# Recurrent stage entered with one block: weights staged in the outputs' memory and split between its first steps; attention's side work moved by a slot or two, its late stores held

## What is computed

```python
def _L0_ffn_ref(x, wf, uf, bf, wi, ui, bi, wc, uc, bc, wo, uo, bo, in_c):
    def step(c, xt):
        ft = jax.nn.sigmoid(xt @ wf.T + c @ uf.T + bf)
        it = jax.nn.sigmoid(xt @ wi.T + c @ ui.T + bi)
        gt = jnp.tanh(xt @ wc.T + c @ uc.T + bc)
        return ft * c + it * gt, None
    c_final, _ = lax.scan(step, c0, x)
    return jnp.tanh(jnp.einsum('tbi,oi->tbo', x, wo) + c_final @ uo.T + bo)

def _L1_attn_ref(x, w_qkv, w_out, head_scales, head_dirs):
    ...
    scores = jnp.einsum('bhqd,bhkd->bhqk', q, k) * SCALE
    scores = jnp.where(causal[None, None], scores, -jnp.inf)
    ...
    attn = jax.nn.softmax(scores + head_scales[None, :, None, None] * geo_bias, axis=-1)
    out = jnp.einsum('bhqk,bhkd->bhqd', attn, v)
    return out.transpose(0, 2, 1, 3).reshape(Bx, Tx, Cx) @ w_out
...
h = _layernorm(x, axis=-1) * (1 + cb) + sb
x = x + gb * _L0_ffn_ref(h, ...)
...
h = _layernorm(x, axis=-1) * (1 + ca) + sa
x = x + ga * _L1_attn_ref(h, ...)
```

## Time and profile before

| | us |
|---|---|
| median of 3 runs | 2527.28 (2520.66 to 2527.5) |
| the profiled execution | 2525.71, span 2523.9 |
| PE busy in it | 2237.5 (89%) |
| DVE / ACT / POOL busy | 1622.1 / 1315.0 / 435.3 |
| recurrent stage, first DMA to last instruction | 664.5 to about 1027 |
| attention, batch loop | 1121 to about 2000 |

### The profile page before, as it was taken

The page is one execution under the profiler, slowest core; times in us unless marked ns, Lnnn a source line. Parts: engine busy times, 40 slices in busy tenths (PEclk is TensorE's granted clock), DMA queues, the critical chain, the costliest instruction groups (busy, mean ns, idle before and its releaser), DMA issues. The chain is left out here.

```text
span 2523.9 us, 44190 instructions
## 1 busy us (share of the span) xinstructions
PE 2237.5 (89%) x14498; PEld 1650.7 (65%) x14498; DVE 1622.1 (64%) x3572; ACT 1315.0 (52%) x2260; POOL 435.3 (17%) x364
## 2 busy tenths in 40 slices
PE   7999999999699999569999999999999692289997
PEld 6766766766488888445666666666666491179986
DVE  4767667666444444676777777777776475856663
ACT  3655655655355555465665666666565460044442
POOL 0000000000011111431111111111111030056663
PEclk8999999999799999789999999999999895589999
DMA  3300000000100000123333332333333067055642
GB/s 111 126 0 0 0 0 0 0 0 0 34 0 0 0 0 0 43 58 90 94 88 78 85 86 81 85 92 93 79 86 86 6 215 229 0 155 133 129 88 32
DMA packets 122974, 156.63 MB, mean 62 GB/s; under 512 B 26896, under 2 KB 104096, under 8 KB 122784
## 3 DMA queue, kind: packets, MB, share of 16 engines
q1 hardware_dynamic: 104480, 129.85, 18.3%
q0 software_dynamic: 14336, 25.44, 5.3%
q10 hardware_dynamic: 4096, 0.53, 0.1%
HBM read 96.26 MB, written 58.98 MB: 62 GB/s over the span
## 5 line engine op out<-in xcount | busy, mean ns | idle before, releaser
L1411 DVE TENSOR_REDUCE at_top<-psum 128x1 f32<-128x512 f32 (+3 forms) x1024 | 461.4, 483 | 224.3 <-PE psum L1128 221.4
L1598 ACT ACTIVATE out_x<-psum 128x512 f32<-128x512 f32 (+1 forms) x768 | 387.8, 531 | 309.8 <-PE psum L1148 286.4
L1144 PE MATMUL psum<-out_x 98*128 98x512 bf16 (+3 forms) x1024 | 267.0, 302 | 18.4 <-DMA out_x<-at_neg_top 15.7
L1124 PE MATMUL psum<-out_x 96*128 96x512 bf16 (+3 forms) x1024 | 266.0, 301 | 15.9 <-DVE at_top L1411 8.0
L1128 PE MATMUL psum<-at_mask_q,at_ident_b 128*128 128x128 bf16 (+1 forms) x768 | 182.9, 238 | 0.0
L1148 PE MATMUL psum<-at_mask_k,at_ident_b 128*128 128x128 bf16 (+1 forms) x768 | 182.7, 238 | 0.0
L1160 PE MATMUL psum<-out_x,at_values 128*32 128x512 f32 (+3 forms) x2048 | 153.0, 440 | 1.5 <-ACT out_x L1598 1.1
L1144 PEld LDWEIGHTS psum<-out_x 98*128 98x128 bf16 x1024 | 90.3, 98 | 87.2 <-issue 38.0
L1124 PEld LDWEIGHTS psum<-out_x 96*128 96x128 bf16 x1024 | 99.2, 99 | 59.4 <-DVE at_top L1411 15.3
L2395 POOL DMA_INDIRECT out<-ex_result,slot_tokens x64 | 119.5, 1867 | 103.6 <-DVE ex_result L2527 89.0
L2573 ACT ACTIVATE ex_mid<-psum,ex_b_up 128x512 f32<-128x512 f32 x96 | 66.2, 690 | 105.4 <-PE psum L61 103.7
(11 more groups left out here) (403 smaller groups left out, 5952.5 us busy)
## 6 DMA issues: line engine op xcount, KB each, us to landing
out_x<-qk_parts SPq DMA_DIRECT2D x128, 192.0 KB
out_x<-qk_parts SPq DMA_DIRECT2D x128, 128.0 KB
qk_parts<-at_q_parts SPq DMA_DIRECT2D x96, 128.0 KB
qk_parts<-at_k_parts SPq DMA_DIRECT2D x96, 128.0 KB
x_residual<-in_x SPq DMA_DIRECT2D x16, 512.0 KB, 3.9
out_x<-qk_parts SPq DMA_DIRECT2D x128, 64.0 KB
token_rows<-ro_h_tok SPq DMA_DIRECT2D x16, 512.0 KB, 3.0
token_rows<-ro_gate_row SPq DMA_DIRECT2D x16, 512.0 KB, 4.1
```

Of the source, the lines that this page charges most:

```text
L1124: pe.matmul(out, q_stack[0:STACK, h, qt * P:(qt + 1) * P], k_stack[0:STACK, h, 0:w], start=(col == 0), stop=True, skip_group_check=(col > 0))
L1144: pe.matmul(bank(bk)[:, col:col + w], k_stack[0:STACK + N_SHIFT, h, kt * P:(kt + 1) * P], q_stack[0:STACK + N_SHIFT, h, kt * P:T], start=( ...
L1411: dve.tensor_reduce(top[:, h, qt:qt + 1], bank(MAX_BANK[f])[:, col:col + w], AX.X, ALU.max).then_inc(mxr.sem, 1)
L1598: act.activation(probs[:, slot(h), 512 * f:512 * f + w], bank(f)[:, 0:w], ACT.Exp).then_inc(ex.sem, 1)
```

## The change

1. The recurrence's first block is gone. SP sends all eight weights, in the order of use (wo, wi, wc, wf, ui, uc, uf, uo), into the last quarter of `out_x`, without waiting for buffers, the small loads after the fourth. Splitting them is written between the first instructions of the steps' block; PE waits for `w_lo` before the first use of each. Layer norm 0 stands first on DVE.
2. Attention: `pe_qk(1)` from (2,0) to (2,1), `pe_turn_o(i, 2)` from (14,2) to (15,0); on DVE the tables RESTS, NORMS and LOWS and `dve_normal(i, 2)`, on ACT PART1 and PART2, each at some entries one to four slots later.
3. SP's third store of a batch also waits until the row maxima of group 2 of the batch before have landed; the fourth store and load groups 1 to 3 stand behind it in SP's queue.

```diff
-        names = ("wf", "wi", "wc", "wo", "uf", "ui", "uc", "uo")
+        names = ("wo", "wi", "wc", "wf", "ui", "uc", "uf", "uo")
...
-            full = [ctx_w.enter_context(nc.sbuf_tensor(f"rc_full{n}", [P, DK, D], F32)) for n in range(4)]
...
+            staged = out_x[:, STEPS - len(names) // 2:, :, :].rearrange("p a k t -> p (a k t)").rearrange(
+                "p (w k n) -> p w k n", w=len(names), k=DK)
...
+            @block.sync
+            def _(sp):
+                for n, name in enumerate(names):
+                    sp.dma_start(staged[:, n, :, :], t[name + "T"].rearrange("(k p) n -> p k n", p=P)
+                                 ).then_inc(loaded[n // 2], 16)
+                    if n == 3:
...
+                if first:
+                    pe.wait_ge(w_lo, 1)
...
+                        elif m == 0:
+                            pe.wait_ge(w_lo, g + 2)
...
                 pe_inputs(pe, 0, True)
+                pe.wait_ge(w_lo, len(names))
...
                 dve_layer_norm(dve, 0, True)
+                dve_w_lo(dve, 0)
+                dve_w_lo(dve, 1)
+                dve_hT_lo(dve, 0)
+                dve_w_lo(dve, 2)
+                dve_w_lo(dve, 3)
+                dve.wait_ge(small, 5 * 16)
+                dve.tensor_copy(c[:, :, :], in_c[:, :].unsqueeze(2).to_broadcast([P, DK, T])).then_inc(c_start, 1)
+                dve_layer_norm(dve, 1, False)
+                for n in range(4, len(names)):
+                    dve_w_lo(dve, n)
+                dve.wait_ge(c_start, 1)
                 dve_c_lo(dve, -1)
-                dve_hT_lo(dve, 0)
-                dve_layer_norm(dve, 1, False)
...
-            if at == (2, 0) and not last:
+            if at == (2, 1) and not last:
                 pe.wait_ge(*neg(i, 2 * N_SHIFT))
                 pe_qk(pe, 1)
...
-            if at == (14, 2):
+            if at == (15, 0):
                 pe.wait_ge(*(hTf(i + 2, DK) if turn else xs(i - 1, 1)))
                 pe_turn_o(pe, i, 2)
...
-            RESTS, STATS = ((1, 2), (2, 2), (3, 1), (4, 1)), ((5, 0), (5, 2), (6, 1), (6, 2))
-            NORMS, LOWS = ((8, 2), (9, 0), (10, 0), (10, 1)), ((13, 2), (14, 2))
+            RESTS, STATS = ((1, 2), (3, 0), (3, 2), (4, 1)), ((5, 0), (5, 2), (6, 1), (6, 2))
+            NORMS, LOWS = ((10, 0), (10, 2), (11, 0), (11, 1)), ((13, 2), (15, 0))
...
-            if at == (15, 0):
+            if at == (15, 2):
                 dve_normal(dve, i, 2)
...
-            PART1, PART2 = ((1, 0), (2, 1), (3, 0), (4, 0)), ((2, 0), (3, 1), (4, 1), (5, 0))
+            PART1, PART2 = ((1, 0), (2, 2), (3, 1), (4, 0)), ((2, 0), (3, 2), (4, 1), (5, 0))
...
             if n == 2 and later:
+                sp.wait_ge(*row[2](b - 1, row[2].per))
                 sp.wait_ge(*loaded[3](b - 1, loaded[0].per))
```

More of the change, by code:

```diff
@@ L729, in signal @@
             return Signal(ctx, nc, "rc_" + name, per, before)
-        with ExitStack() as ctx_w:
-            full = [ctx_w.enter_context(nc.sbuf_tensor(f"rc_full{n}", [P, DK, D], F32)) for n in range(4)]
[L733 to L765, removed]
         with ExitStack() as ctx:
@@ L776, in recurrent_stage @@
             gates = [sb2(ctx, nc, f"rc_gate_{n}", [P, DK, T]) for n in ("forget", "input", "new")]
+            in_c = sb2(ctx, nc, "rc_in_c", [P, DK])
+            staged = out_x[:, STEPS - len(names) // 2:, :, :].rearrange("p a k t -> p (a k t)").rearrange(
+                "p (w k n) -> p w k n", w=len(names), k=DK)
             F, I, G = 0, 1, 2
+            loaded = [ctx.enter_context(nc.semaphore(f"rc_loaded{n}")) for n in range(len(names) // 2)]
+            small, w_hi, w_lo, c_start = (ctx.enter_context(nc.semaphore("rcw_" + n)) for n in ("small", "hi", "lo", "start"))
             def sig(name, per=1, before=0):
@@ L799, in recurrent_stage @@
             block = ctx.enter_context(nc.Block())
+            @block.sync
[4 more added lines that the diff above has]
+                    if n == 3:
+                        for j, b in enumerate(("bf", "bi", "bc", "bo")):
+                            sp.dma_start(bias[:, j, :], t[b]).then_inc(small, 16)
+                        sp.dma_start(in_c[:, :], t["in_c"]).then_inc(small, 16)
             def pe_turn(pe, i, first):
@@ L874, in dve_layer_norm, with dve_w_lo @@
                                       ALU.subtract, ALU.mult).then_inc(s_xn.sem, 1)
+            def dve_w_lo(dve, n):
+                hi, lo = w[names[n]]
+                dve.wait_ge(w_hi, n + 1)
+                dve.tensor_tensor(lo[:, :, :], staged[:, n, :, :], hi[:, :, :].bitcast(F32), ALU.subtract).then_inc(w_lo, 1)
             def dve_hT_lo(dve, i):
@@ L932, in _, with act_w_hi @@
                 pool_new(pool, STEPS - 1)
+            def act_w_hi(act, n):
+                if n % 2 == 0:
+                    act.wait_ge(loaded[n // 2], 32)
+                act.activation(w[names[n]][0][:, :, :], staged[:, n, :, :], ACT.Copy).then_inc(w_hi, 1)
             def act_hT(act, i):
@@ L973, in _ @@
             def _(act):
+                act_w_hi(act, 0)
+                act_w_hi(act, 1)
+                act_hT(act, 0)
+                act_w_hi(act, 2)
+                act_w_hi(act, 3)
+                act.wait_ge(small, 5 * 16)
+                act_out(act, 0)
+                for n in range(4, len(names)):
+                    act_w_hi(act, n)
+                act.wait_ge(c_start, 1)
                 act_c_hi(act, -1)
-                act_hT(act, 0)
-                act_out(act, 0)
                 with act.Fori(0, STEPS - 1) as i:
```

## The result

| | before | changed |
|---|---|---|
| median, us | 2525.2 (2520.66 to 2532.37, 6 runs) | 2509.3 (2505.91 to 2511.41, 6 runs) |
| span of the profiled execution, us | 2523.9 | 2507.0 |

The ratio is 0.9934, interval 0.9923 to 0.9945: the kernel became faster, by 15.9 us where 35.8 were forecast. The time lies inside the range, but 19.9 us of the forecast did not come, and most of them are the one term of 15.9 us that the second rival takes away.

What follows compares the result with a forecast made beforehand. TensorE (PE), busy 89% of the span, was taken as the bound, so its standstills counted. Terms 14.2 + 15.9 + 6.4 + 0 - 0.7 = 35.8 us off 2525.7 or the median 2527.28 gave 2491, range 2474 to 2512.

Steps and rivals of the forecast that it cites:

- the second rival: Attention loop: PE's wait for the maxima stays, behind load group 0, or reappears at (12,0); 15.9 us less, 2507; chance 0.22.
- Entry: Start of the recurrent stage: without the first block and its barrier, layer norm and first product start 14.2 us earlier.
- late weights: Recurrent stage's start: weights landing and being split too late for the first product; cost 0 to 1.1 us, taken 0.
- Held stores: Attention, (8,0): with third and fourth store held, group 2's maxima land in time; 1.06 us a batch, 15.9 in 15.
- row wait: Attention loop, (8,0): PE waits for row maxima that come by DMA, 12.6 us in 14 batches.
- The forecast batch of 54.2 us: Attention loop: sign expected in the changed profile, a batch of some 54.2 us, 1.5 less than before.
- The arbitration rule: DMA engines alternate between queues after every packet, so SP's backlog should delay ACT's small transfer little; holding stores brings nothing.
- Cost of the hold: SP's queue in attention: load group 1 begins near 1539 instead of 1536.45, wanted 13 us later; cost 0.
- End of a batch: Waits at (14,2) and (0,1) go, but DVE's normalization then decides; 0.46 of 1.50 us kept, 14 times: 6.4.
- Slots (2,0) to (3,2): Attention: `pe_qk(1)` loses its wait of 0.34 + 0.16 us, `pe_qk(3)` at (3,2) waits 0.5 instead; net 0.
- NORMS: Attention, DVE: two normalizing instructions moved later; no gain at (10,1), possible small wait at (12,2), 0.05 us a batch: -0.7.
- Sum: Whole kernel: all terms together save 35.8 us, 14.2 + 15.9 + 6.4 + 0 - 0.7.

## Why the prediction was wrong, point by point

- **Entry (14.2)**: right. 14.2 by the traces, 13.4 (8.6 to 18.2) by the ratio of the run of the entry alone, 12.1 by its medians. The choice of 0 for late weights was right: ACT begins the first split at 666.83, 4.4 us ahead of the split of `rc_hT` (671.28).
- **Held stores (15.9)**: this is the step that failed. The prediction had both bounds, and took the upper one "since the packets slow down when the stores come". The number of packets per us fell when the stores came, but it falls in the same way when none come: 2 and 6 per us in the changed kernel. What fits all the runs is that the maxima's last packets wait on the few engines that still have the broadcast loads to do: with load group 0 held they land after 1.7 us, with it spread after 3.5 at most. Two things coincided, the stores and the end of what the other engines had to do, and I read the nearer as the cause. The earlier trace rows begins with the maxima's issue at 1530.20 and leaves out what was issued ahead of it. The condition that the second rival names (load group 0, right before) was the true one; its price, 15.9 less, too. "Against: the earlier trace rows" was the misreading. Where the row wait is really taken away, it gives 18.4 (kernel before) and 21.3 us, of which 3.8 and 4.3 are the first load of the stage. The forecast batch of 54.2 us shows the same: from one batch's maxima to the next it is 55.7 before, 55.4 in the changed kernel and 54.3 with the loads spread (means of 13 batches).
- The arbitration rule of the prediction gave the right sign for the hold. The Trainium skill (DMA: Bandwidth & Descriptors, "Queues, rings and completion order") says of the unit that an engine drains before it turns to the next queue that it is a packet of typically 9 to 17 descriptors; the prediction took it for one of the trace's small packets, and so concluded that no backlog could hold up the maxima by much. If a turn holds 16 runs of 4 KB it can; no run here shows how long a turn is. The same page ("Why a DMA increments its semaphore by 16 and not by 1") says that the engines of a DMA are the largest number up to 16 that divides the slowest dimension over 1 of both sides, and that the lowest-numbered are taken; for these loads that would be 3 and 2, starting at the same one. The trace has no engine numbers, but its share of 15 to 19% and the spread loads agree with the small numbers of engines. That both loads start at the same engine is shown by no run.
- **Cost of the hold (0)**: too low. 3.28 us at (12,0) of the first batch. The prediction said that group 3's maxima have slack "as wide as group 2's"; in the first batch they have not.
- **End of a batch (6.4)**: mechanism right, size too large. The walk also counts from 1506.05, where the earlier trace rows gives 1506.11 (1505.69 + 0.42); with that it would have kept 0.40 a batch, 5.6. The waits at (14,2) and (0,1) went and the value product at (0,2) waits for the normalization instead. The distance from `pe_out` at (10,1) to this value product, in the changed kernel:

```profile
1474.83 0.50 PE L59 MATMUL psum<-at_o_hi,at_wo_hi 128*128 128x512 f32 x1 [0.64 <-DVE out_x L1453]
...
1493.94 1.39 PE L1171 MATMUL psum<-out_x,at_values 128*32 128x512 f32 x12 [0.29 <-DVE out_x L1453]
```

  is 19.11; in the kernel before that `pe_out` starts here:

```profile
1490.14 0.50 PE L59 MATMUL psum<-at_o_hi,at_wo_hi 128*128 128x512 f32 x1 [0.64 <-DVE out_x L1442]
```

  and the product at 1509.46, 19.32. 0.21 a batch is kept, not 0.46: 2.9 us. Part of it is a new gap of 0.18 at (0,0) for which the trace names no releaser.
- **Slots (2,0) to (3,2) (0)** and **NORMS (-0.7)**: the exchange of 0.34 for 0.38 is as forecast, and no wait came at (12,2). All slots together were forecast at 5.7 and measured at 5.5, the difference of two medians whose intervals are some 5 us wide; so the size is only roughly confirmed. The NORMS step left (10,1) at 0.64, as argued from the earlier trace rows; the runs on DVE's order show that this wait is set by the place of the normalization itself.
- **Sum**: by the medians the runs give 12.1 + 5.5 - 2.4 = 15.2, by the ratio of the entry 16.5, against 15.9 measured. These are steps of one chain from before to changed, so their sum has to come near; it shows where the gain lies, and that no 15.9 for the stores is in it.

## What to carry to other kernels

When a small transfer lands late, look at what was issued before it as well as behind it, and at the share of the engines beside the number of packets: few packets at a share of 15 to 20%, with large DMAs still under way, pointed here to a backlog on two or three engines. What helped was to cut the large DMAs, not to move other transfers away. Look at the landings of the group in question, too: a median over all of them hid that half of the cutting had left its delay nearly whole. Before a wait is added, ask what the trace would look like if the suspect were innocent; here the trickle of packets would have looked the same. A wait for a step of DVE is moved by the step's own place in DVE's order, and one slot may not be enough: the wait of 9.2 us at (10,1) became 4.4 by one slot and left the list by two.

## What was unexpected of the hardware

- Behind a load of 768 KB, two of whose six DMAs read a broadcast source, a transfer of 64 small packets lands after 7.2 to 7.4 us. With the same bytes in nine DMAs none lands later than 3.5 (median of all 1.7), and three more issues a group on SP's queue cost nothing that can be seen.
- With waits of 2.8 us once a batch PE's granted clock had a mean of 0.97 in the loop, where with waits of about 1 us it was 1.00, and the edit cost 40 us where its waits explain 25.
